# Sharing the attention products between VectorE and ScalarE in the last eleven steps

## The reference

```python
xl = (x @ W_l).reshape(N, HEADS, HEAD_DIM)
xr = (x @ W_r).reshape(N, HEADS, HEAD_DIM)
e = xl[src] + xr[dst]
e = jnp.where(e >= 0, e, NEG_SLOPE * e)
score = jnp.einsum('ehd,hd->eh', e, att)
m = jax.ops.segment_max(score, dst, num_segments=N)
ex = jnp.exp(score - m[dst])
denom = jax.ops.segment_sum(ex, dst, num_segments=N)
alpha = ex / (denom[dst] + SM_EPS)
agg = jax.ops.segment_sum(alpha[:, :, None] * xl[src], dst, num_segments=N)
```

## Time and profile before

| what | us |
|---|---|
| runs: median (lowest, highest) of 3 | 1543.99 (1532.38, 1544.35) |
| the profiled execution | 1535.07 |
| its span, first to last instruction | 1533.0 |
| TensorE busy in the span | 1186.2 |
| VectorE busy in the span | 1033.3 |
| ScalarE busy in the span | 863.7 |
| ScalarE, first to last product of the attention (starts) | 223.1 to 1114.4 |

### The profile page before, as it was taken

How to read it: one execution, slowest core, us unless ns; L and a number is a source line. 1 busy time by engine, 2 the same in 40 slices (tenths; PEclk the granted TensorE clock), 3 DMA queues, 4 the chain that set the end, 5 groups by cost and what they waited for, 6 DMA issues and landing times. The chain is left out here.

```text
span 1533.0 us, 25022 instructions
## 1 busy us (share of the span) xinstructions
PE 1186.2 (77%) x5749; PEld 857.7 (56%) x5749; DVE 1033.3 (67%) x2176; ACT 863.7 (56%) x3334; POOL 784.0 (51%) x872
## 2 busy tenths in 40 slices
PE   7677568888888888888888898888679808999920
PEld 4345346666666666666666676666446705555510
DVE  5562578899899989999989998999348500000037
ACT  2231017888887878878878888888922302232211
POOL 5000777777777777777777777775051050000034
PEclk9788789999999999999999999999876558999965
DMA  5430667778777777777778777875060022352213
GB/s 150 155 128 1 166 177 191 198 206 201 198 201 199 204 194 195 204 194 194 202 194 204 195 202 197 202 201 139 32 187 1 1 85 67 90 148 83 82 52 94
DMA packets 161308, 230.32 MB, mean 150 GB/s; under 512 B 36484, under 2 KB 134141, under 8 KB 160829
## 3 DMA queue, kind: packets, MB, share of 16 engines
q1 hardware_dynamic: 121284, 124.33, 29.1%
q0 software_dynamic: 37056, 102.46, 26.6%
q10 hardware_dynamic: 2880, 2.66, 0.5%
HBM read 186.36 MB, written 42.99 MB: 150 GB/s over the span
## 5 line engine op out<-in xcount | busy, mean ns | idle before, releaser
L1107 POOL DMA_INDIRECT e_xl<-d_xl,e_idx x704 | 670.6, 953 | 228.5 <-issue 198.1
L1401 ACT ACTIVATE e_prod<-e_xl,e_prod 128x64 f32<-128x64 f32 x2816 | 691.4, 334 | 5.7
L1362 PE MATMUL bank<-e_prod,e_selt 128*128 128x260 f32 x1408 | 362.5, 403 | 53.3 <-ACT e_prod L1401 30.2
L1362 PEld LDWEIGHTS bank<-e_prod,e_selt 128*128 128x128 f32 x1408 | 272.6, 199 | 107.8 <-issue 44.8
L1314 PE MATMUL bank<-e_xr,e_sel 128*128 128x256 bf16 x2112 | 299.0, 279 | 9.1 <-DVE e_sel L1124 7.7
L1319 PE MATMUL bank<-e_xl,ident 128*128 128x256 f32 x704 | 224.1, 401 | 80.5 <-DMA e_xl<-d_xl,e_idx 80.0
L1314 PEld LDWEIGHTS bank<-e_xr,e_sel 128*128 128x128 bf16 x2112 | 208.8, 100 | 84.3 <-issue 10.8
L1149 DVE TENSOR_REDUCE e_score<-e_edge 128x16 f32<-128x1024 f32 x176 | 212.4, 1207 | 0.3
L1319 PEld LDWEIGHTS bank<-e_xl,ident 128*128 128x128 f32 x704 | 108.3, 194 | 106.2 <-DMA e_xl<-d_xl,e_idx 102.4
L1810 DVE COPY f_y<-bank 98x256 f32<-98x256 f32 (+1 forms) x32 | 11.3, 416 | 226.9 <-PE bank L1781 226.9
L1132 DVE TENSOR_TENSOR e_edge<-bank,e_xl 128x512 f32<-128x512 f32 x176 | 119.4, 678 | 27.6 <-PE bank L1319 27.5
(11 more groups left out here) (314 smaller groups left out, 1104.8 us busy)
## 6 DMA issues: line engine op xcount, KB each, us to landing
e_xr<-d_xr SPq DMA_DIRECT2D x176, 192.0 KB
d_hist<-e_acc SPq DMA_DIRECT2D x176, 130.0 KB
e_drow<-d_rel SPq DMA_DIRECT2D x176, 128.0 KB
w_rows<-in_L_ffn_w_dram SPq DMA_DIRECT2D x16, 1024.0 KB, 7.7
e_xl<-d_xl,e_idx POOLq DMA_INDIRECT x704
e_rows<-d_rows SPq DMA_DIRECT2D x22, 192.5 KB
d_xr<-a_xr SPq DMA_DIRECT2D x20, 192.0 KB
d_in<-zero SPq DMA_DIRECT2D x3, 1024.0 KB
```

Of the source, the lines that this page charges most:

```text
L1107: pool.indirect_dma_start(xl[:, q.slot * G + g, :], None, m.d_xl, bass.IndirectOffsetOnAxis(ap=idx[p][:, at:at + 1], axis=0)).then_inc(gat ...
L1362: last = pe.matmul(ps_agg[b], selt[:, b, g, :], flat(prod[:, b, g, :, :]), start=(g == 0), stop=(g == G - 1))
L1401: last = act.activation(prod[:, b, g, h, 0:HEAD], xl[:, q.slot * G + g, h * HEAD:h * HEAD + HEAD], ACT.Copy, scale=prod[:, b, g, h, HEAD:H ...
```

## The change

From quad 165 on (`SHARED`), the last eleven that are weighed, ScalarE forms only the products of groups 0 and 1 (8 instructions) and VectorE those of groups 2 and 3, in one instruction (`share_weights`), after the exponential of that quad. VectorE does it at the end of its step. TensorE waits for both before the first of the four groups. All steps before are as they were.

```diff
@@ -952,6 +952,7 @@
 CLOSE_LAG = WEIGH_LAG + 1
 SPREAD_LAG = WEIGH_LAG - 1
 STORE_LAG = CLOSE_LAG + 4
+SHARED = QUADS - WEIGH_LAG
 
 
 class Quad:
@@ -995,7 +996,7 @@
 
 
     sb = lambda name, shape, dt=F32: ctx.enter_context(nc.sbuf_tensor(name, shape, dt))
-    s = sem_set(nc, m.sems, "att", "init idx sel edges summed relu score lin turned run top ends heads fwd bwd carried drop cols raised tops topped diff rr f fac ex prod selt agg old acc rows* links fixed")
+    s = sem_set(nc, m.sems, "att", "init idx sel edges summed relu score lin turned run top ends heads fwd bwd carried drop cols raised tops topped diff rr f fac ex prod selt agg old acc rows* links fixed shares")
     loaded = [m.sems.enter_context(nc.semaphore(f"att_loaded{r}")) for r in range(4)]
     stored = [m.sems.enter_context(nc.semaphore(f"att_stored{r}")) for r in range(4)]
     gathered = [m.sems.enter_context(nc.semaphore(f"att_gathered{r}")) for r in range(RING)]
@@ -1173,6 +1174,13 @@
 
 
 
+
+            def share_weights(q):
+
+                b = q.slot % 2
+                dve.wait_ge(s["ex"], q.k + 1)
+                dve.tensor_tensor(prod[:, b, 2:4, :, 0:HEAD], xl[:, q.slot * G + 2:q.slot * G + 4, 0:DIM].rearrange("p g (h c) -> p g h c", h=HEADS),
+                                  prod[:, b, 2:4, :, HEAD:HCOLS].to_broadcast([P, 2, HEADS, HEAD]), ALU.mult).then_inc(s["shares"], 1)
 
             def linear(o):
                 p = o.slot // RUN
@@ -1295,6 +1303,9 @@
                     less_tops(o)
                 if live:
                     scores(q)
+                v = q.ago(WEIGH_LAG)
+                if v.known() and SHARED <= v.k < QUADS:
+                    share_weights(v)
             for k in range(2):
                 select(Quad(0, k))
             over_quads(dve, quad, behind=CLOSE_LAG)
@@ -1358,6 +1369,8 @@
                 if q.since(2):
                     pe.wait_ge(s["acc"], q.k - 1)
                 pe.wait_ge(s["prod"], q.k + 1)
+                if q.known() and q.k >= SHARED:
+                    pe.wait_ge(s["shares"], q.k - SHARED + 1)
                 for g in range(G):
                     last = pe.matmul(ps_agg[b], selt[:, b, g, :], flat(prod[:, b, g, :, :]), start=(g == 0), stop=(g == G - 1))
                 last.then_inc(s["agg"], 1)
@@ -1396,7 +1409,7 @@
                     act.wait_ge(s["agg"], q.k - 1)
                 act.activation(prod[:, b, :, :, HEAD], diff[:, p, :, q.at * G:q.at * G + G].rearrange("p h g -> p g h"), ACT.Exp).then_inc(s["ex"], 1)
                 act.wait_ge(s["ex"], q.k + 1)
-                for g in range(G):
+                for g in range(2 if q.known() and q.k >= SHARED else G):
                     for h in range(HEADS):
                         last = act.activation(prod[:, b, g, h, 0:HEAD], xl[:, q.slot * G + g, h * HEAD:h * HEAD + HEAD], ACT.Copy,
                                               scale=prod[:, b, g, h, HEAD:HCOLS])
```

## The result

The changed kernel takes 1549.35 us (median of 20 runs, 1535.29 to 1554.38), the kernel before 1540.22 (20 runs, 1532.31 to 1547.67): 1.0056 times as long, 95% interval 1.0034 to 1.0078, so 5 to 12 us longer. Runs of one and the same kernel differ by 15 to 19 us, so only the interval counts here.

A forecast was written before the change was run, and what follows sets the result against it. Bound taken: the chain of ScalarE's products, TensorE's group matmuls and VectorE's addition. Full clock gave -1.7 us, two slow bursts +2.8, together +1.1 on the median of 1543.99: 1545 us, range 1531 to 1555.

The forecast's parts named there:

- rival C: TensorE stays at half clock once there: all ten of quads 166 to 175 slow +16 us, half +8; chance 0.23.
- Who bounds the tail after the change: End of the attention, to the last addition of sums: TensorE would wait for VectorE's product instead of ScalarE's.
- gap and step: Last quads: 1.87 us from one TensorE burst to the next; with a burst of 1.99, 3.86 us per quad.
- the ring: Last quads: TensorE's burst, then VectorE's addition, selector and product follow one another without overlap, 3.86 us against 4.09.
- The product's price: VectorE's one multiplication of 128x512 floats per step: taken as 0.68 us, bounds 0.36 and 0.75.
- The carried columns behind the burst of quad 166: Their transposes queue on TensorE behind that burst, so the columns VectorE waits for come 1.91 us later.
- The sum at full clock: Last addition of sums at 1116.10 us against 1117.80: 1.70 us gained if no burst is slow.
- I therefore count two slow bursts at 1.41: 2.8 us: Bursts of quads 166 and 167, behind TensorE's longer pauses, run at lowered clock, adding 1.41 us each.
- excess: TensorE's burst time beyond 1.99 us each: 5.1 us over the old tail's nine bursts, mostly hidden under ScalarE's step.
- after that the pauses are 1.87 us, so I expect mostly full clock: TensorE's bursts after quads 166 and 167: pauses shorter than the 2.1 us of now, so mostly full clock.
- forecast A: The forecast case: two or three slow TensorE bursts in the tail, +1 to +5 us; chance 0.5.

The follow-up runs named there:

- Runs 4 and 7: Each against the changed kernel: 4, TensorE waits for VectorE's products only ahead of its third group, 1530.06 us; 7, VectorE's product ahead of the selector, 1536.09 us.
- run 3: Against the changed kernel, VectorE forms its products ahead of its addition of the quad before, for all eleven quads; 1521.55 us.
- Run 5: The changed kernel with TensorE's pauses in the tail filled by extra matmuls that leave the output untouched; 1534.8 us.
- run 8: The changed kernel once more, nothing altered, for a second profile; 1549.73 us.
- run 11: The kernel before, with extra matmuls on TensorE in the part behind the attention (the routing); 1541.8 us.

## Why the prediction was right, and what it missed

The direction was right, and the measured median lies in the range; the size was not. I had +1.1 us, the measured difference is +8.6 (+5.2 to +12.0). That 1549.35 lies in 1531 to 1555 says little for the sum: the range is 24 us wide, from the spread of executions and the +11 of rival C. And 1545 looks nearer than it was, since the median of three runs of before that I started from, 1543.99, was 3.8 us above that of 20.

- **Who bounds the tail after the change.** Right. ScalarE idles, TensorE waits for VectorE's product 11 times, and gap and step are 1.87 and 3.86 us as worked out. Runs 4 and 7 take a part out of the ring and the step falls by that part (0.94 and 0.60); run 3 takes the ring away and the step falls to 2.31.
- **The product's price.** 0.68 taken, 0.682 measured. The 0.67 us row that I gave as an operation "from SBUF" has one input in a PSUM bank, and so has the selector; the product, with both in SBUF, took as long.
- **The carried columns behind the burst of quad 166.** Right, and larger: they come 15.7 us after the last score reduction instead of 10.6 (1085.35 and 1079.00 for the copy), 5.1 us later, of which 1.9 were forecast. The rest is the clock.
- **The sum at full clock.** 1.70 us less than before. Run 5 has the change at nearly full clock: 50.15, less 1.7 of the one slow burst and 0.7 of the fill, is 47.7, which was the forecast.
- **The step that failed: "I therefore count two slow bursts at 1.41: 2.8 us".** The excess was 7.1 us in the first profile and 7.8 and 7.7 in two others of the same tail (run 8, and the change with the routing filled), in five or six bursts, most of them 1.4 to 1.8 each. I had left out quad 165, whose burst comes 2.5 us after a lone transpose and was slow in two of the three, and I had taken 1.41, the excess of a burst that recovered on the way, for all. And "after that the pauses are 1.87 us, so I expect mostly full clock" holds only from quad 170 on in two of the profiles, and from 172 on in the third. My own rows spoke against it: of the 5.1 us of excess in the kernel before, 3.7 came from three bursts of the steady beat, behind pauses of 1.1 to 2.1 us, 2.98 us after 2.09, 3.77 after 1.10 and 2.93 after 2.08. With 7.1 in the place of 2.8 my sum gives -1.7 + 7.1 = +5.4; the tail measured +5.6. That lies 0.6 above the +1 to +5 of my forecast A and 2.4 below the +8 at which rival C had half of the bursts slow. By the number of slow bursts, five or six of eleven, C is nearer, but TensorE didn't stay at half clock as C has it: it came back in all three profiles while the pauses stayed 1.87 us. What brings it back is open.
- **Tail and total.** The tails of the three profiles (55.0, 55.4, 55.8) are 5.6 to 6.3 us longer than the 49.44 of before, and 3.6 to 4.4 longer than the 51.43 of run 11; the measured difference is 5.2 to 12.0. Its two profiles have a routing of 105.7 and 107.7 us, but so has the kernel before with its tail filled (107.2), and run 5, with the change's own order, has 97.4. So the long routing isn't peculiar to the change. The times of the runs suggest that the change has it more often: an execution less its tail and its routing leaves 1384 to 1390 us in all 13 profiles. With its tail and a routing of under 99 us the changed kernel would thus take at most 1545, and 17 of its 20 runs took longer; the kernel before would take at most 1540 (with the 51.43 of run 11), and 10 of its 20 took longer, 42 of the 99 in all comparisons. With the tail filled (run 5) 4 of 12 ran over that bound, 1539 there. An estimate from these counts: the long routing in 35 to 45 more of 100 executions, at 7 to 9 us each, is 2.5 to 4 us on the mean; with the 5.6 to 6.3 of the tail that makes 8 to 10, and 8.6 was measured. This is worked out and not shown: no run without a profile tells in which part it spent its time, and what would make the routing long more often stays open.

## What to carry to other kernels

Work given to a second engine helps only if that engine can do it while the consumer is busy with the item before. Put it ahead of any instruction that waits for the consumer: here the same 0.68 us product makes the tail 5.6 us longer behind the addition and 16.0 us shorter ahead of it (8.6 us lost and 12.9 gained in the whole kernel, by the ratios). Before adding a wait, list what stands behind it on the waiting engine (here the carried columns) and what was hidden under the old bound: slow bursts that cost 1 to 3 us under ScalarE's step cost 7 in the ring.

## What the runs showed of the hardware

In the ring the same pattern, a burst and 1.87 us of idle time, ran at either clock: in the changed kernel the burst of quad 169 took 3.81 us after such a pause, and the six of quads 170 to 175 took 1.99 after the same pause or a shorter one; in run 8 two bursts of 3.80 stand just ahead of the first of 1.99. So the length of a pause alone doesn't tell the clock of the next burst. The matmuls and transposes of the routing ran with TensorE recorded as busy for over 90% of the time in two profiles, and yet at a granted clock of 0.62 to 0.67 on the mean (of 2.4 GHz, its levels being 1.2 and 2.4); from 1215 to 1230 us of the changed kernel's profile it is recorded as busy without a break at 0.50. That part took between 97.4 and 110.2 us in 13 profiles of nearly the same instructions.
